# A graph-network kernel on one core: one of four row tiles scattered one stage earlier, and GpSimd's program written out chunk by chunk

## What is computed

```
h = relu(layernorm(x))
x1 = x + GAT(h)      # x_l = h W_l + b_l, x_r = h W_r + b_r; per edge and head a score of
                     # leaky_relu(x_l[src] + x_r[dst]); softmax over the edges into a node
                     # and its own self loop; sum of alpha * x_l[src]; + bias
h = relu(layernorm(x1))
x2 = x1 + CF(h)      # per edge: msg = (h W_in)[dst] * (ssp(attr Wf1 + bf1) Wf2 + bf2) * weight,
                     # summed by src; then two dense layers per node
```

## Time and profile before

| | |
|---|---|
| time, median of 3 runs (lowest, highest) | 3588.07 us (3582.42, 3593.24) |
| span of the profiled execution, first to last instruction | 3550.3 us |
| median time less that span | 37.8 us |
| busy: PE, DVE, ACT, POOL | 82%, 75%, 64%, 53% of the span |
| mean granted clock of TensorE | 0.918 |
| attention stage, 98 chunks | one step about 12.0 us |
| message stage, 98 chunks | one step about 13.2 us |

### The profile page before, as it was taken

How to read it: one execution, slowest core, us unless ns; L and a number is a source line. 1 busy time by engine, 2 the same in 40 slices (tenths; PEclk the granted TensorE clock), 3 DMA queues, 4 the chain that set the end, 5 groups by cost and what they waited for, 6 DMA issues and landing times.

```text
span 3550.3 us, 60748 instructions
## 1 busy us (share of the span) xinstructions
PE 2925.4 (82%) x16576; PEld 1746.4 (49%) x16576; DVE 2674.8 (75%) x7105; ACT 2271.7 (64%) x4705; POOL 1874.7 (53%) x1583
## 2 busy tenths in 40 slices
PE   3999968888888888897777777777777775999999
PEld 2666644444444444443444444444444443666665
DVE  5888859999999999999676676667667664444454
ACT  3999956666666666665555555555555553888887
POOL 0000046666666666663688888888888886000000
PEclk9999989999999999999877888878888887999999
DMA  4767733333333333333455555555555555777776
GB/s 169 254 246 251 248 112 121 122 125 112 125 125 110 127 122 112 126 122 104 105 109 108 108 108 112 108 106 110 108 108 108 111 107 116 278 291 291 294 294 236
DMA packets 280365, 545.65 MB, mean 154 GB/s; under 512 B 96723, under 2 KB 173037, under 8 KB 242639
## 3 DMA queue, kind: packets, MB, share of 16 engines
q1 hardware_dynamic: 186255, 447.94, 37.2%
q0 software_dynamic: 94080, 97.34, 15.4%
HBM read 317.71 MB, written 235.91 MB: 156 GB/s over the span
## 4 chain that ended last, share of the span: by engine, by line
DVE 30%; issue 21%; PE 18%; POOL 12%; ACT 9%; DMA 9%; SPq 1%; POOLq 1%; DVEq 0%; ACTq 0%
POOL sum_dram L567 7%; PE bank L1368 6%; ACT d_n L983 6%; PE bank L1359 5%; POOL x_dram L555 4%; DMA b_x<-x_end_dram 4%; DVE a_sum L818 3%; DVE a_max L780 3%; PE bank L1174 3%; DMA x_dram<-b_x,sidx 3%; DVE stat_e_six L750 2%; DVE a_nd L761 2%; DVE a_pv L812 2%; PE bank L1208 2%; PE bank L1365 2%
## 5 line engine op out<-in xcount | busy, mean ns | idle before, releaser
L529 POOL DMA_INDIRECT a_xs<-in_x,gidx x392 | 399.6, 1019 | 589.7 <-issue 589.7
L567 POOL DMA_INDIRECT sum_dram<-b_sum,b_at x392 | 616.6, 1573 | 137.8 <-issue 118.6
L535 POOL DMA_INDIRECT a_xd<-in_x,gidx x392 | 408.8, 1043 | 241.4 <-DVE a_base L797 150.6
L555 POOL DMA_INDIRECT x_dram<-b_x,sidx x392 | 443.3, 1131 | 158.8 <-issue 138.4
L934 DVE SCALAR_TENSOR_TENSOR f_ssp_out<-bank,cols,f_ln_out 128x512 f32<-128x512 f32 x196 | 147.1, 751 | 295.2 <-ACT f_ln_out L1082 295.2
L597 ACT ACTIVATE stat_e_log<-stat_e_var 128x8 f32<-128x8 f32 (+1 forms) x196 | 40.5, 207 | 507.3 <-DVE stat_e_var L593 507.3
L850 DVE BATCH_NORM_STATS2 stat_e_six<-b_x 128x6 f32<-128x128 f32 x392 | 85.5, 281 | 357.1 <-DMA b_x<-x_end_dram 357.1
L1328 PE MATMUL bank<-b_rows,b_same 128*128 128x128 bf16 x4704 | 331.8, 240 | 0.2 <-ACT b_sum L1125 0.2
L1328 PEld LDWEIGHTS bank<-b_rows,b_same 128*128 128x128 bf16 x4704 | 317.0, 110 | 0.3 <-issue 0.3
L983 ACT ACTIVATE d_n<-d_x,stat_d_shift,stat_d_rstd 128x128 f32<-128x128 f32 x686 | 283.5, 485 | 0.2 <-DVE stat_d_shift L603 0.2
L1174 PE MATMUL bank<-ident,d_n 128*128 128x128 f32 x1568 | 229.6, 275 | 43.9 <-DMA d_n<-sum_dram 29.5
(11 more groups left out here) (174 smaller groups left out, 7193.6 us busy)
## 6 DMA issues: line engine op xcount, KB each, us to landing
d_x<-in_x SPq DMA_DIRECT2D x49, 1024.0 KB, 6.8
x_dram<-d_x SPq DMA_DIRECT2D x49, 1024.0 KB, 4.8
d_n<-sum_dram SPq DMA_DIRECT2D x49, 1024.0 KB, 6.9
d_x<-x_dram SPq DMA_DIRECT2D x49, 1024.0 KB, 8.8
out<-d_x SPq DMA_DIRECT2D x49, 1024.0 KB, 4.9
sum_dram<-zero SPq DMA_DIRECT2D x48, 1024.0 KB, 5.5
x_end_dram<-a_x SPq DMA_DIRECT2D x98, 256.0 KB, 3.5
b_x<-x_end_dram SPq DMA_DIRECT2D x98, 256.0 KB
```

The lines of the kernel that those rows point to most:

```text
L529: pool.indirect_dma_start(a_xs[s][:, j * F:(j + 1) * F], None, x, bass.IndirectOffsetOnAxis(ap=gidx[s][:, j:j + 1], axis=0)).then_inc(src_ ...
L535: pool.indirect_dma_start(a_xd[s][:, j * F:(j + 1) * F], None, x, bass.IndirectOffsetOnAxis(ap=gidx[s][:, 4 + j:5 + j], axis=0)).then_inc( ...
L555: pool.indirect_dma_start(x1_dram, bass.IndirectOffsetOnAxis(ap=sidx[s][:, j:j + 1], axis=0), b_x[s][:, j * F:(j + 1) * F], None, bounds_c ...
L567: pool.indirect_dma_start(sum_dram, bass.IndirectOffsetOnAxis(ap=b_at[s][:, j:j + 1], axis=0), b_sum[s][:, j * F:(j + 1) * F], None, compu ...
```

## The change

- `EARLY = (1, 1)`: of each chunk's four row tiles of x1, the first is scattered into `x1_dram` in the attention stage, straight from `a_x1`, behind the gathers of the chunk four further on. The other three are scattered in the message stage as before.
- POOL's program has no loops any more: all 98 chunks of both stages are written out. Its indices are taken from the table `index` directly, so the loads of `gidx` and `sidx` on SP go away.
- POOL waits for the stores of the dense stage (`x1_stored`) before its first gather, and no longer before its first scatter. DVE, before it writes `a_x1` again, and SP, before the message stage, wait for `early_scattered` as well.

```diff
+EARLY = (1, 1)
-        gidx = [sb(f"gidx{i}", [P, 8], I32) for i in range(2)]
-        sidx = [sb(f"sidx{i}", [P, 4], I32) for i in range(2)]
+        def late(s):
+            return 16 * (TILES - EARLY[1 - s])
@@ SP, before the message stage and in it
                 sp.wait_ge(end_stored[s], 16 * HALF)
+                sp.wait_ge(early_scattered[s], 16 * EARLY[s] * HALF)
-                    sp.wait_ge(x1_scattered[s], 64 * turn(k, u - 2))
+                    sp.wait_ge(x1_scattered[s], late(s) * turn(k, u - 2))
-                sp.dma_start(sidx[s][:, :], index[:, bass.ds(12 * (NC - 1 - t) + 8, 4)]).then_inc(b_sidx_ld[s], 16)
@@ POOL
+            def early_scatters(t):
+                s = t % 2
+                pool.wait_ge(x1_ready, t + 1)
+                pool.sem_inc(pool_step, 1)
+                for j in range(EARLY[s]):
+                    pool.indirect_dma_start(x1_dram, column(t, 2 * TILES + j), a_x1[s][:, j * F:(j + 1) * F], None,
+                                            bounds_check=bound, oob_is_err=False).then_inc(early_scattered[s], 16)
             for i in range(RN):
                 pool.wait_ge(x1_stored[i], 16 * in_slot[i])
+                pool.sem_inc(pool_step, 1)
+            for t in range(NC + 4):
+                if t < NC:
+                    gathers(t)
+                if t >= 4:
+                    early_scatters(t - 4)
             pool.wait_ge(cleared, 16 * NG)
+            def scatters(t):
+                s = t % 2
+                pool.wait_ge(b_x_ld[s], 16 * (t // 2 + 1))
                 pool.sem_inc(pool_step, 1)
+                for j in range(EARLY[1 - s], TILES):
+                    pool.indirect_dma_start(x1_dram, column(NC - 1 - t, 2 * TILES + j), b_x[s][:, j * F:(j + 1) * F], None,
                                             bounds_check=bound, oob_is_err=False).then_inc(x1_scattered[s], 16)
+            for t in range(NC + 2):
+                if t < NC:
+                    scatters(t)
+                if t >= 2:
+                    adds(t - 2)
@@ DVE
                         dve.wait_ge(end_stored[s], 16 * turn(k, u - 4))
+                        dve.wait_ge(early_scattered[s], 16 * EARLY[s] * turn(k, u - 4))
```

More of the change, by code:

```diff
@@ L282, in gnn, with early @@
         ROUNDS = (NG - 1 - RX) // RX
+        def early(s):
+            return EARLY[s] * F
+        def late(s):
+            return 16 * (TILES - EARLY[1 - s])
         def node_rows(a, g):
@@ L408, in _ @@
             for u in range(5):
-                step_a(HALF - 1, u, 4 + u, gather=False, keep=u < 2)
+                step_a(HALF - 1, u, 4 + u, keep=u < 2)
             clear(HALF - 1)
@@ L461, in _ @@
             for s in range(2):
[L462 removed]
+                sp.wait_ge(x1_scattered[s], late(s) * HALF)
                 sp.wait_ge(added[s], 64 * HALF)
@@ L517, in _, with column @@
             pool.wait_ge(store_setup, 96)
-            def gathers(k, u, t0):
-                s = u % 2
-                pool.wait_ge(gidx_loaded[s], 16 * turn(k, u))
-                if t0 >= 2:
-                    pool.wait_ge(norm_src, 2 * k + u - 1)
-                pool.sem_inc(pool_step, 1)
-                for j in range(TILES):
-                    pool.indirect_dma_start(a_xs[s][:, j * F:(j + 1) * F], None, x,
-                                            bass.IndirectOffsetOnAxis(ap=gidx[s][:, j:j + 1], axis=0)).then_inc(src_gathered[s], 16)
-                if t0 >= 2:
-                    pool.wait_ge(base_ready, 2 * k + u - 1)
+            def column(t, n):
+                return bass.IndirectOffsetOnAxis(ap=index[:, 12 * t + n:12 * t + n + 1], axis=0)
@@ L533, in gathers @@
+            def gathers(t):
+                s = t % 2
+                if t >= 2:
+                    pool.wait_ge(norm_src, t - 1)
                     pool.sem_inc(pool_step, 1)
                 for j in range(TILES):
-                    pool.indirect_dma_start(a_xd[s][:, j * F:(j + 1) * F], None, x,
-                                            bass.IndirectOffsetOnAxis(ap=gidx[s][:, 4 + j:5 + j], axis=0)).then_inc(dst_gathered[s], 16)
-            for u in range(4):
-                gathers(0, u, u)
@@ L540, in _ @@
-            with pool.Fori(2, HALF) as k:
-                for u in range(2):
-                    gathers(k, u, 4)
+                    pool.indirect_dma_start(a_xs[s][:, j * F:(j + 1) * F], None, x, column(t, j)).then_inc(src_gathered[s], 16)
+                if t >= 2:
+                    pool.wait_ge(base_ready, t - 1)
+                    pool.sem_inc(pool_step, 1)
+                for j in range(TILES):
+                    pool.indirect_dma_start(a_xd[s][:, j * F:(j + 1) * F], None, x, column(t, TILES + j)).then_inc(dst_gathered[s], 16)
@@ L553, in scatters, with adds @@
                 pool.sem_inc(pool_step, 1)
-                for j in range(TILES):
-                    pool.indirect_dma_start(x1_dram, bass.IndirectOffsetOnAxis(ap=sidx[s][:, j:j + 1], axis=0),
-                                            b_x[s][:, j * F:(j + 1) * F], None,
+                for j in range(EARLY[1 - s], TILES):
+                    pool.indirect_dma_start(x1_dram, column(NC - 1 - t, 2 * TILES + j), b_x[s][:, j * F:(j + 1) * F], None,
                                             bounds_check=bound, oob_is_err=False).then_inc(x1_scattered[s], 16)
-            def adds(k, u, first=False):
-                s = u % 2
-                pool.wait_ge(b_at_ready, 2 * k + u + 1)
-                pool.wait_ge(b_sum_ready, 2 * k + u + 1)
-                if not first:
-                    pool.wait_ge(added[1 - s], 64 * turn(k, u - 1))
-                pool.sem_inc(pool_step, 1)
+            def adds(t):
+                s = t % 2
+                pool.wait_ge(b_at_ready, t + 1)
+                pool.sem_inc(pool_step, 1)
+                pool.wait_ge(b_sum_ready, t + 1)
+                pool.sem_inc(pool_step, 1)
+                if t:
+                    pool.wait_ge(added[1 - s], 64 * ((t - 1) // 2 + 1))
+                    pool.sem_inc(pool_step, 1)
@@ L568, in adds @@
                                             b_sum[s][:, j * F:(j + 1) * F], None, compute_op=ALU.add).then_inc(added[s], 16)
-            for u in range(4):
-                scatters(0, u)
-                if u >= 2:
-                    adds(0, u - 2, first=u == 2)
-            with pool.Fori(2, HALF) as k:
-                for u in range(2):
-                    scatters(k, u)
-                    adds(k, u - 2)
-            for u in range(2):
-                adds(HALF, u - 2)
+            for t in range(NC + 2):
+                if t < NC:
+                    scatters(t)
+                if t >= 2:
+                    adds(t - 2)
         def statistics(dve, st, n, six_done, sumdif_done, sq_done, var_done, at, count):
```

26 lines of the change are left out of this document (8 added, 18 removed).

## The result

The changed kernel takes 3824.16 us in the median (3822.48 to 3825.37, 4 runs) against 3590.65 us: a ratio of 1.066, interval 1.064 to 1.067. It is slower by 233.5 us; 3468 us were forecast, and the range was 3440 to 3500. (Some executions of a kernel are slower at a lower granted clock; where a kernel has both, the fast ones are compared.)

What follows compares the result with a forecast made beforehand. DVE was taken to bound the attention stage and POOL's eight DMAs the message stage. The sum 3550.3 - 122.1 + 0 + 1.5 = 3429.7 us, with 37.8 us added, gave 3468 us; range 3440 to 3500.

Steps and rivals of the forecast that it cites:

- It has 1.30 us to spare: Attention stage: POOL would do its eight gathers in 10.71 us of DVE's 12.01 us step.
- I price it at nothing: Attention stage: with one more scatter POOL needs 11.995 us against DVE's 12.01, so the scatter costs 0.
- Rival B: Attention stage: POOL becomes the pace, DVE waiting for `a_xd`; up to 24 us, total 3492; chance 0.22.
- Message step 11.93 us: Message stage: one scatter and gap less takes 1.285 us from 13.22; 122.1 us over 95 steps, POOL still the bound.
- POOL's load in the attention stage: Attention stage: gathers 4 x 1.047 + 4 x 1.022 us busy, plus an early scatter at the cheapest row, 0.98 us.
- the 3492 us: Attention stage: by the skill's port rule the early scatter is paid at the dear price, total 3492 instead of 3468.
- DVE's wait for `b_x`: Message stage: DVE's pause in each step falls from 3.93 to about 2.6 us.
- rival E: Whole written-out program: each POOL DMA dearer, at 0.083 us each 124 us together, total 3592; chance 0.05.
- 3429.7 us of span: Whole kernel: profiled span 3550.3, less 122.1 in the message stage, plus 0 in attention and 1.5 at the borders.
- 37.8 us: Whole kernel: median of the runs above the profiled span, for what stands before and behind it and the runs' spread.

Runs made afterwards that it cites:

- e4: Changed kernel with semaphores declared so they keep the numbers of the kernel before, first kind of chip: 3446.65 us, 0.9689 of the kernel before.
- e2: Kernel before, loops and index loads kept, plus only the early scatter, first kind of chip: 3437.17 us, 0.9663 of the kernel before.
- e7: Changed kernel with EARLY = (0, 0), written out but no early scatter, second kind of chip: 3579.47 us, 1.0008 of the kernel before.
- e1: Changed kernel with EARLY = (0, 0), written out but no early scatter, first kind of chip: 3553.79 us, 0.9997 of the kernel before.
- e5: Changed kernel unedited, on a chip of the second kind: 3866.65 us, 1.0748 of the kernel before.
- e10: Changed kernel unedited, on another chip of the second kind: 3782.29 us, 1.0566 of the kernel before.
- e15: Written-out program, six forms of POOL's attention step in turn, all four tiles scattered in the message stage, second kind: 3876.77 us, one run; kernel before 3593.66.
- e3: Changed kernel with the loads of gidx and sidx as before, first kind of chip: 3439.10 us, 0.9668 of the kernel before.
- e12: Changed kernel, POOL waiting behind each early scatter for its landing, first kind of chip: 3676.51 us, 1.0340 of the kernel before.
- e13: Changed kernel with EARLY = (1, 0), POOL waiting behind each early scatter for the chunk's gathers, first kind of chip: 3609.54 us, 1.0152 of the kernel before.
- e14: Changed kernel, POOL waiting behind each early scatter for the chunk's gathers, first kind of chip: 3583.10 us, 1.0077 of the kernel before.
- part 6 of e15: Chunks 84 to 97: early scatter, then a fill by POOL of 0.99 us; step 14.35 us over 13 chunks, 13.3 in the calm 7.
- e6: Same text as e4, the changed kernel with the old semaphore numbers, on a chip of the second kind: mean 3846.95 us, 1.072 of the kernel before.
- e16: Changed kernel with EARLY = (1, 0) and a 128x512 fill by POOL behind each chunk's DMAs, second kind: 3641.95 us, 1.0142 of the kernel before.
- parts 1, 2 and 5 of e15: Forms without a break: ninth gather, early scatter, scatter that skips nearly all rows; steps 16.34, 16.33 and 15.58 us.
- parts 3 and 4: Forms with the early scatter and a break, of 2.1 us, or of 1.0 and 2 us; steps 14.72 and 13.97 us.

## Why the prediction was wrong

**The step that failed** is in the attention stage: "It has 1.30 us to spare", and with it "I price it at nothing" for the early scatter. In the sum of durations the pause was free. On a chip of the second kind it was not: without it the engines stop for about 8 us in 32, and the attention stage costs 385 us more instead of 0. Rival B had the right place, POOL's lost slack, but as a price of 24 us at most; no rival held a loss that is larger than the work added. The range was built from durations of instructions, and this cost is in none of them.

**What was right**, by its own steps:
- Message step 11.93 us: measured 12.06 over 90 steps (e4: 12.15), from 13.24 before. So a step gained 1.18 us (e4: 1.09) where 1.285 were put down, and the stage 114.1 us (e4: 106.4) of 122.1. The plain step did what was said, 12.00 us in the median from 13.22. The rest is in steps with an unusually long indirect DMA: 11 of the 90 steps lie more than 0.5 us above the median (e4: 18, e2: 5) where the kernel before has 2. Why is open. The additions became 1.588 us from 1.570.
- POOL's load in the attention stage: 4 x 1.047 + 4 x 1.022 + 0.98 = 9.26 us forecast, (346.1 + 318.4 + 107.5)/83.3 = 9.27 us in e4, step 12.01 us in both. The early scatter was a dear one, 1.295 us, and the gathers behind it became cheaper by as much, 0.959 from 1.022. The scatter's own row, beside a VectorE that is 98% busy, agrees with the rule of the Trainium skill (SBUF — State Buffer, "SBUF: two separate sides") that certain VectorE operations make GpSimd's descriptor writes wait. The longer step and the 3492 us that the prediction worked out beside it did not come.
- DVE's wait for `b_x`: 3.8 us in the mean before (353.9 us, 93 times), 2.6 us after (229.5 us, 88 times), 2.6 forecast.
- The written-out program costs nothing (rival E): 0.9997 and 1.0008. That agrees with the Trainium skill (Runtime: NRT & Kernel Launch, "Instruction fetch mechanics"), by which the fetch of straight code is mostly hidden.
- Early scatter and message stage together, on a chip of the first kind: 0.9689 in e4. The sum said 3429.7 us of span; e4's span is 3446.1, 16.4 more, nearly all of it the message stage's missing gain. That e4's time, 3446.65 us, lies only 21 us from the 3468 is partly luck: the span was 16 us too short, and what was put on top of it (next paragraph) some 36 us too much.

**A second error lay in reading the inputs.** The prediction put 37.8 us "before the first and behind the last instruction". In the runs here the time is about 2 us above the span of the same execution (3822.48 and 3820.7). The profiled span of before, 3550.3 us, fits a chip of the first kind, and its median, 3588, one of the second. So the whole working was read from a trace of the kind on which no stop was seen. Its weak form was visible on chips of the second kind only: e7 there loses against e1 12 us in the attention stage (first scatter of the message stage 1698.16 against 1685.77), behind POOL's first 20 gathers in a row (and 18 us in the message stage: over 90 steps POOL has 21 indirect DMAs above 1.9 us there where e1 has 2, and is busy 989.1 us instead of 972.3; why is not explained).

**What stays open.** Why signals of PE come late while POOL issues gathers in a row was not found, nor what differs between the chips. A break and a lower mean pace of POOL's DMAs were never separated: every break spreads the DMAs too. Two things bound the cause. The message stage has POOL without a pause for over 1000 us, one DMA in 1.72 us where the attention stage has one in 1.33 us, and its stops are far smaller. In the result's trace, of the second kind, it has none to speak of, 12.06 us a step against 12.15 in e4 on the first kind. But it is not free of them: in e5, the same program on another chip of the second kind, ACT's `b_sum` waited 39 times for an unknown releaser, 137.4 us together and up to 4.3 us, and the step was 12.90 us; in e10 it was 19 times, 68.5 us and 12.47 us. One of these waits, in e5:

```profile
2614.23 0.60 ACT L1128 ACTIVATE b_sum<-bank 128x512 f32<-128x512 f32 x1 [3.67 <-remote]
```

Whether the pace of the DMAs, their kind or the other engines' work makes the difference between the stages was not tried. And what the ninth DMA moves is not it: the stops are there with a gather, with a scatter and with a scatter that skips nearly all rows (e15). The DMA engines' share is lower with stops, 0.29, than without, 0.37, but that follows from the longer stage and shows nothing by itself.

No version here beats both kernels on both kinds. e2, the early scatter with the loops left as they were, is the best on the first, with e3 beside it (3437.17 and 3439.10 us, 0.966 and 0.967), and as bad as the change on the second (1.0709). The kernel before is the best known on the second.

## What to carry to other kernels

Slack of an engine is free in the sum of durations only; where a change is to use up the last pause of an engine that issues DMAs, put that case, with a price beyond the sum, among the rivals, and time it on more than one chip. A break that is put back is not free where it delays the gathers for which the pacing engine waits: in e12, e13 and e14 DVE waited 1.1 to 2.2 us a chunk for them. When the time and the span of a profile differ by more than runs of one kernel do among themselves, the two may be from different chips, and the trace may not show what the timed one does. Several forms of a step in one written-out program, chunk range by chunk range, let one execution compare them on one chip; it is then one execution of each, and a form can inherit its start from the one before (part 6 of e15).

## What the hardware showed that was not expected

- Two kinds of chips for one program: 3446.65 and 3846.95 us for the same text (e4, e6), where the kernel before differs by 1% (3555.95 and 3589.14).
- While POOL issues indirect gathers in a row, one each 1.33 us, ACT and DVE on the second kind start up to 10.9 us behind the end of the product of PE that they wait for, where 1.2 and 1.65 us are usual; DVE's signal reached PE in 0.06 us in the same stop. Most of the long waits end about 2 us behind the row; shorter ones of about 3 us end within it. Where a delay begins is less sure: a long wait often starts 16.35 us into the row, but that is where ACT runs out of other work, and single waits began at 9 to 15 us. DMA-free breaks of 0.7 to 2 us in every chunk (e15, e16) take away most of it; no least length is shown.
- PE's granted clock falls with the stops: 0.82 to 0.84 in parts 1, 2 and 5 of e15, 0.93 and 0.94 in parts 3 and 4, where the attention stage of the kernel before has 0.99.
